# A one-core embedding, attention and expert kernel: first group's rows gathered apart, embeddings moved to later slots, squares in halves, first expert weights rounded in quarters

## What is computed

```python
emb = word_table[ids] + (domain_table[dom] @ proj_w.T + proj_b) + type_table[kind] + pos_table[pos]
h = layer_norm(emb, gamma, beta)                      # 32 sequences x 128 tokens x 192
x = layernorm(h)                                      # "magnitude" attention, 12 heads of 16
sr, si = (qr@kr + qi@ki) * scale, (qi@kr - qr@ki) * scale
h = h + softmax(sqrt(sr*sr + si*si)) @ v
h = h + causal_attention(layer_norm(h)) @ proj + b    # ordinary causal attention
h = h + mixture_of_experts(layer_norm(h))             # 8 experts, top 2, capacity 1280 rows each
```

## Time and profile before

| | |
|---|---|
| median of 3 runs | 1126.58 us (1125.38 to 1136.05) |
| the profiled execution | 1129.93 us |
| its span, first to last instruction | 1128.1 us |
| busy, share of the span | PE 83%, weight loads 63%, ACT 60%, DVE 59%, POOL 41% |
| mean granted TensorE clock | 0.908 of full speed |

### The profile page before, as it was taken

One profiled execution on the slowest core, in us unless ns is written; L12 is line 12 of the kernel. 1 busy time (PEld: TensorE's weight loads), 2 busy tenths in 40 slices (PEclk: granted clock), 3 DMA queues, 4 the chain that ended last, 5 costly groups with the idle time before them and its releaser, 6 DMA issues.

```text
span 1128.1 us, 21988 instructions
## 1 busy us (share of the span) xinstructions
PE 934.3 (83%) x7210; PEld 713.2 (63%) x7210; DVE 665.4 (59%) x3058; ACT 673.0 (60%) x1339; POOL 464.4 (41%) x508
## 2 busy tenths in 40 slices
PE   1234888879888979999999999946999999999996
PEld 1222555556555556666666666535888888889896
DVE  1344889879887766676766656374433434433332
ACT  2013888877888877887787778435443443443431
POOL 6666465444000110223222212213476676676654
PEclk7565999999999969999999998655999999999999
DMA  7233232232011100011011012143473455474352
GB/s 196 42 59 54 58 66 38 50 60 37 19 29 24 35 2 1 2 34 34 2 34 34 4 32 62 34 82 34 88 110 68 89 110 75 78 114 74 53 56 28
DMA packets 64259, 59.23 MB, mean 53 GB/s; under 512 B 17534, under 2 KB 55328, under 8 KB 64160
## 3 DMA queue, kind: packets, MB, share of 16 engines
q0 software_dynamic: 26112, 27.89, 18.0%
q1 hardware_dynamic: 38048, 30.12, 10.3%
HBM read 35.28 MB, written 16.39 MB: 46 GB/s over the span
## 4 chain that ended last, share of the span: by engine, by line
PE 55%; DVE 14%; ACT 11%; issue 7%; POOL 6%; DMA 4%; SPq 2%; ACTq 0%; POOLq 0%; DVEq 0%
PE ps_scores L724 13%; PE ps_ring L716 9%; PE ps_ring L965 7%; PE ps_ring L724 6%; POOL got L547 4%; PE ps_scores L965 4%; PE ps_scores L839 4%; ACT square L1061 3%; PE ps_ctx L856 3%; PE ps_scores L842 3%; SPq L458 2%; DVE probs L1329 2%; DMA got<-place_rows,id_now 2%; PE ps_ring L796 1%; ACT prob_t L1054 1%
## 5 line engine op out<-in xcount | busy, mean ns | idle before, releaser
L598 POOL DMA_INDIRECT out<-z_t,slots_now x80 | 135.3, 1692 | 102.1 <-DVE z_t L1624 83.0
L1168 ACT ACTIVATE probs<-ps_scores,fc_bias 128x512 f32<-128x512 f32 (+1 forms) x144 | 88.3, 617 | 146.9 <-PE ps_scores L724 143.7
L1054 ACT ACTIVATE prob_t<-ps_ring 128x512 f32<-128x512 f32 x192 | 113.8, 595 | 34.9 <-PE ps_ring L716 32.9
L716 PE MATMUL ps_ring<-ident,probs 128*128 128x128 f32 x768 | 127.8, 292 | 5.6 <-DVE x_hi L1222 2.5
L1061 ACT ACTIVATE square<-ps_scores 128x1024 f32<-128x1024 f32 x96 | 98.3, 1024 | 45.5 <-PE ps_scores L839 44.3
L1329 DVE CUSTOM_DVE_ANT_0 probs<-ps_scores,causal 128x128 f32<-128x128 f32 x384 | 88.8, 286 | 58.4 <-PE ps_scores L842 58.0
L1077 ACT ACTIVATE probs<-probs,neg_max 128x128 f32<-128x128 f32 x384 | 120.7, 395 | 3.6 <-DVE neg_max L1329 3.6
L965 PE MATMUL ps_ring<-work,probs 128*128 128x192 f32 x672 | 115.9, 328 | 5.6 <-ACT probs L1168 5.4
L1323 DVE CUSTOM_DVE_ANT_0 probs<-square 128x128 f32<-128x128 f32 x384 | 89.0, 286 | 46.2 <-ACT square L1061 43.1
L965 PEld LDWEIGHTS ps_ring<-work,probs 128*128 128x128 f32 x672 | 109.2, 190 | 9.4 <-issue 9.4
L724 PE MATMUL ps_scores<-x_hi,fc_hi 128*128 128x512 f32 (+1 forms) x288 | 105.1, 370 | 7.4 <-DVE x_hi L1608 4.8
(11 more groups left out here) (211 smaller groups left out, 2207.3 us busy)
## 6 DMA issues: line engine op xcount, KB each, us to landing
k<-k_signed SPq DMA_DIRECT2D x192, 32.0 KB
work<-pj_w SPq DMA_DIRECT2D x8, 576.0 KB, 4.4
token_in<-xin SPq DMA_DIRECT2D x8, 384.0 KB, 3.5
out<-resid SPq DMA_DIRECT2D x8, 384.0 KB, 4.3
vals<-fc_w SPq DMA_DIRECT2D x8, 384.0 KB, 3.4
vals<-fc_w SPq DMA_DIRECT2D x16, 192.0 KB, 4.2
out<-z_t,slots_now POOLq DMA_INDIRECT x80, 3.6
token_in<-xin SPq DMA_DIRECT2D x8, 128.0 KB, 4.3
```

The costliest lines, as they stand in the source:

```text
L598: gp.indirect_dma_start(out[:, :], bass.IndirectOffsetOnAxis(slots_now[:, u, 1, t:t + 1], 0), slot_y[:, o, :], None, compute_op=ALU.add).t ...
L716: return pe.transpose(dst, src, ident[0:n, 0:n])
L1054: sc.activation(prob_t[:, s % 2, :, :], src.rearrange("p (h q) -> p h q", h=4), ACT.Exp if p is mag else ACT.Copy).then_inc(ring_free[i], 1)
L1168: sc.activation(hidden[:, c % 2, f_, 0:128 * nt], ps_scores[:, i, 0:128 * nt], ACT.Gelu, bias=fc_bias[:, e, f_:f_ + 1]).then_inc(gelu_done ...
```

## The change

It does eight things. (1) The first group's position and domain rows are gathered without adding, into the two halves of the `square` tile, so no kind waits for the one before; DVE adds the three together (two 128x768 additions). (2) `id_now` has two buffers and the word gathers of the next group no longer wait for the last domain rows. (3) SP loads the causal weights only once the first group's domain rows have landed. (4) `EMBED_LATE` moves DVE's embedding steps of groups 1, 2, 3, 4 later by 9, 9, 5 and 2 slots, their "xT" fills with them, and gives group 1 its projections at slots 9 to 13 of pass 0. POOL's norms move to slots 4 and 6 for groups 0 and 1, and to slots 4 and 12 for all others. (5) The first group's keys are moved with 8 DMAs of all three blocks instead of 24. (6) ACT squares each job in two instructions of two heads, each with its own wait and its own release. (7) The first expert's weights are rounded and their remainder made in quarters, in slots 3 to 6 and 5 to 8 of pass 16. (8) `LAST_LAGS` is one slot later for all but "keep".

```diff
-XT_SLOT = {"mag": (0, 1), "cau": (1, 2)}
+XT_SLOT = {"cau": (1, 2)}
+EMBED_LATE = (0, 9, 9, 5, 2, 0, 0, 0)
+EARLY_PROJ, EARLY_VALUE = {1: (9, 10, 10, 11, 12, 13)}, {0: (14, 15), 1: (14, 15)}
-SPLIT_SLOT = 4
+SPLIT_SLOT = 3
+def magnitude_fills(at, g):
+    fills = back_fills(at - STEPS)
+    first = max(0, EMBED_LATE[g] - 2)
+    fills += [("xT", k) for k in range(2) if at == first + k - STEPS]
+    fills += [("proj", k) for k in range(6) if at == EARLY_PROJ.get(g, MAG_PROJ)[k] - STEPS]
+    return fills + [("value", k) for k in range(2) if at == EARLY_VALUE.get(g, MAG_VALUE)[k] - STEPS]
+def embedding_due(p, slot):
+    for g in range(GROUPS):
+        at = STEPS * (p - g + 2) + slot - EMBED_LATE[g]
+        if 4 <= at <= 13:
+            return g, at
+    return None, None
-LAST_LAGS = {"ctx": 4, "ctxT": 5, "out": 7, "scale": 7, "norm": 9, "zT": 10, "keep": 11, "logits": 12}
+LAST_LAGS = {"ctx": 5, "ctxT": 6, "out": 8, "scale": 8, "norm": 10, "zT": 11, "keep": 11, "logits": 13}
...
+                if done is cau_w_loaded:
+                    sp.wait_ge(dom_got, 16 * GROUP)
...
-            for g in range(GROUPS):
+            sp.wait_ge(keys_signed, BLOCKS)
+            for quarter, part in product(range(4), range(2)):
+                to, of = 32 * quarter + HEAD_DIM * part, 32 * quarter + HEAD_DIM * (1 - part)
+                sp.dma_start(k_of[0][to:to + HEAD_DIM, :, 1, :, :].rearrange("p b s k -> p b (s k)"),
+                             k_signed[of:of + HEAD_DIM, :, :]).then_inc(first_turned, 16)
+            for g in range(1, GROUPS):
...
                 if slot == 0:
-                    if g > 0:
-                        pool.wait_ge(dom_got, 16 * GROUP * g)
                     if g > 1:
+                        pool.wait_ge(dom_got, 16 * GROUP * (g - 1))
                         pool.wait_ge(mag.named("emb_affine0"), g)
...
-                    if slot == 4:
+                    if slot == 4 and g == 0:
+                        pool.wait_ge(place_stored, 16 * KINDS)
+                    elif slot == 4:
                         pool.wait_ge(word_got, 16 * GROUP * (g + 1))
-                        if g == 0:
-                            pool.wait_ge(place_stored, 16 * KINDS)
-                    gather(place_rows, g, slot - 4, place_got, 2, ALU.add)
+                    if g == 0:
+                        gather(apart_from_word[0], place_rows, g, slot - 4, place_got, 2, ALU.bypass)
+                    else:
+                        gather(place, place_rows, g, slot - 4, place_got, 2, ALU.add)
...
             def embedding_norm(p, g, slot):
-                first, second = (2, 5) if p < 0 else (5, 11)
+                first, second = (4, 6) if g < 2 else (4, 12)
...
-                act.wait_ge(mag.scores_full, 2 * (JOBS * g + j) + 2)
-                sc.activation(square[:, j % 2, :, :, :].rearrange("p h m k -> p h (m k)"),
-                              ps_scores[:, :, 0:256], ACT.Square).then_inc(mag.scores_free, 2)
+                for pair in range(2):
+                    act.wait_ge(mag.scores_full, 2 * (JOBS * g + j) + pair + 1)
+                    h = slice(2 * pair, 2 * pair + 2)
+                    sc.activation(square[:, j % 2, h, :, :].rearrange("p h m k -> p h (m k)"),
+                                  ps_scores[:, h, 0:256], ACT.Square).then_inc(mag.scores_free, 1)
...
+            def first_weights_high(quarter):
+                act.wait_ge(raw_loaded, 48)
+                c, some = quarter // 2, slice(FF // 2 * (quarter % 2), FF // 2 * (quarter % 2) + FF // 2)
+                sc.activation(fc_hi[:, 0, c, some], raw_fc[:, c, some], ACT.Copy).then_inc(first_high, 1)
...
-                    if (p, slot) == (2 * GROUPS, SPLIT_SLOT):
-                        expert_weights_high(0, 0)
+                    if p == 2 * GROUPS and 0 <= slot - SPLIT_SLOT < 4:
+                        first_weights_high(slot - SPLIT_SLOT)
...
                 if slot == 4:
+                    if g == 0:
+                        dve.wait_ge(word_got, 16 * GROUP)
+                        rows_, whole = got[:, 0:GROUP * HID], (place_got, dom_got)
+                        for u in range(2):
+                            dve.wait_ge(whole[u], 16 * GROUP)
+                            ve.tensor_tensor(rows_, rows_, first_got[u], ALU.add).then_inc(rows_added, 1)
+                            dve.wait_ge(rows_added, u + 1)
...
-                    if coming is not None and coming < GROUPS:
-                        embedding_step(coming, slot)
-                    elif coming is not None:
+                    g, at = embedding_due(p, slot)
+                    if g is not None:
+                        embedding_step(g, at)
+                    if coming is not None and coming >= GROUPS:
                         causal_input_step(coming - GROUPS, slot)
```

60 lines of the change are left out of this document (39 added, 21 removed).

## The result

| kernel | median, us | of runs | ratio to before | 95% interval |
|---|---|---|---|---|
| before | 1125.98 | 4 | | |
| changed | 1110.73 | 4 | 0.9858 | 0.982 to 0.9896 |

The change makes the kernel faster by 15.3 us, 1.4%. The forecast was a gain of 33 us; 1110.73 lies 0.7 us above the upper end of its range.

A forecast was written before the change was run, and what follows sets the result against it. No engine fills a steady pass; waits around a loop set it, DVE nearest to a bound, and a chain of waits delays the start. -38 + 5 + 10 - 10.5 + 0 = -33.5 us, predicted 1093, range 1078 to 1110.

The forecast's parts named there:

- First group's rows: Ahead of pass 0: last gather starts at 20.9, group 0's statistics at 26.7 instead of 33.8, PE's first product at 41.0.
- Group 0's keys: Ahead of pass 0: last signed copy at 47.3, eight key DMAs landed at 54.9, so scores may start at 55.
- rival C: Group 0's key DMAs: 8 with three times the issue time, scores not before 65; total 1100 us, chance 0.09.
- Pass 0: First magnitude pass: first maximum at 58.0, length 34.3 us, pass 1's at 92.3 instead of 130.4; gain 38, bounds 32 and 43.
- What the later passes give back: Passes after pass 0 and the end: effects of lateness +5, POOL's order +10, halved squares -10.5, the end 0 us.
- (a): After pass 1's first maximum: about 5 us of postponed DVE work is paid back as the lateness falls from 9 to 0.
- (b): POOL's second norm behind the gathers: 13 us of DVE waits in later passes, 10 of them lost; bounds 0 and 15.
- (c): Squares by halves: seven passes gain 1.5 us each, 10.5 together; bounds 0 and 3 a pass, 1 lost at worst.
- (d): The end: weight rounding in quarters and the last group's later lags change 0 us, bounds -1 and +2.
- A: Rival: the gather order on POOL costs nothing; gain 43.5 us, total 1083, chance 0.17.
- B: Rival: halves bring nothing and all waits for POOL's norms bite in full; gain 18 to 22 us, total 1106, chance 0.20.
- D: Rival: DVE's new waits idle PE, its clock falls to 1.2 GHz in magnitude passes; slower, 1144 us, chance 0.02.

The follow-up runs named there:

- the run with the norm early: On the changed kernel, POOL's second norm of groups 2 to 7 at slot 8, ahead of the next group's domain gathers, instead of slot 12: 1104.8 us.

## Why the prediction was wrong, point by point

**First group's rows: right, 1.7 late.** Gathers at 0.95 and 0.30 of issue, the last at 21.2. The statistics came at 28.4 for 26.7: DVE's weight remainders lasted until 26.5 here (24.5 taken over from the earlier trace rows), and only then came the additions, which took 1.94 for the 2.2 taken and waited for no landing. The remainders came late because ACT rounded the weights 2.0 later than before, at 22.2 for 20.2:

```profile
22.24 1.48 ACT L1037 ACTIVATE w_hi<-probs 128x1536 fp32r<-128x1536 f32 x1 [10.49 <-issue]
```

SP issued the loads of these weights only 0.4 later (15.3 for 15.0); where the other 1.6 went was not tried.

**Group 0's keys: 3 us more.** 15 products took until 50.2 with the last copy, for 47.3: 1.6 of it from the start, the rest from a slow clock that lasted from 42.6 to 47.8 and not 3.5 us. The eight DMAs took 5.24, 0.65 each, so rival C (three times the issue for three times the size) is out. But the last of them took 4.43 to land where the 32 KB one of the earlier trace rows took 3.15, 1.3 of the 4.4 by which the keys were late. The Trainium skill (DMA: Bandwidth & Descriptors, Anatomy of one DMA — SWDGE (gpsimd) path) fits 2.0 us and bytes over 436 GB/s to transfers issued from GpSimd; for 96 KB that is 2.2 us, an estimate. These transfers are from SP, and 4.43 was measured on them: the fit does not carry over.

**Pass 0: the step that failed.** "With the 4.5 us that DVE idles in a steady pass, and 1 for the slower clock, it lasts 34.3." It lasts 41.6: 7.3 of the 17.7 that are missing. The sum took the busy time of the engine that is busiest in a steady pass and added the steady pass's idle. But between the jobs of pass 0 DVE does not set the pace, it idles 10.7 of 29.8: PE is busy 26.9, and scores and squares give the first jobs one every 1.7 to 2.6 us. The tail of 11.8 follows in any case. The shortest intervals and the shortest tail of passes 0 to 6 of all the kernels, though of passes with other work, would make 34.6 together, more than the 34.3. Without the early products the pass is 37.3. The other 4.3 are the early products of group 1 between the last jobs (intervals of 3.6, 3.2 and 6.1); that is shown by a run. The other 3.0 are argued from the rows: PE and ACT pace the jobs there, and how much of that is the clock, for which the sum has 1, stays open. I had counted PE's work as at most 29.6 and looked no further, and it came to 33.2; 3.2 of the 3.6 come with the halves alone (32.8 in pass 0 of that run). The view that would have told this is the windows of the earlier trace rows cut once more, at the last job's maximum.

**What the later passes give back.** Forecast -5, -10 and +10.5 from pass 1 on, together -4.5; measured 27.4 at pass 1 and 15.8 at the first causal maximum, -11.6. Of the terms: (a) DVE's payback 5, measured 4.9. (b) POOL's order 10, measured 6 (the run with the norm early): DVE waits 4.1 in passes 1 and 3, where 5.5 and 3.7 stood, and not in pass 4. (c) the halves 10.5, measured 11.1 by the median of the run without them and 8.8 by that of the halves alone; in passes 1 to 7 of the traces 9.6 and 5.9. What no term held is the rest of the lateness: 17.5 minus 4.9 minus 5.6 is 7.0 us of waits in passes 1 to 3, a term that the sum does not have. 4.4 of them go with less lateness once POOL's order is mended, by one pair of traces, and 2.4 by another. PE's part in them is seen in pass 1: the late fill of the transposed input stands in mid-pass ahead of scores, PE waits with DVE (4.2), and the granted clock is 0.86 in place of 1.00. (d) 0, measured 0. So (b) was put 4 us too high, which by luck covered part of the missing 7.0.

ACT's side of the halves came cheaper than I had it. Group by line of the changed kernel (count, busy us, mean ns, idle before):

```profile
L1101 ACT ACTIVATE square<-ps_scores 128x512 f32<-128x512 f32 x192 | 104.8, 601 | 29.0 <-PE ps_scores L877 25.3
```

96 squares of 1.02 make 98.3, so 96 more instructions cost 6.5 us, not the 16 of my rows: of two halves back to back the second begins before the first has ended. By their mean the 192 halves sum to 115.4, and ACT is busy 104.8: an overlap of 0.11 a pair. The Trainium skill (ScalarE: Activation LUTs, What ACT_TABLE_LOAD costs) has back-to-back instructions overlap by about 93 ns, and the estimate of 9 from it was nearer; the trace agrees with the overlap.

**The rivals.** A (POOL's order is free) is refuted by the 4.1 us waits. B came closest in its number (1106), and by luck: it had the halves bring nothing, and they brought more than any other part that was tried. C is out, as said. D holds in a small way: the clock of passes 1 to 3 is 0.86, 0.96 and 0.92 where it was 1.00, 1.00 and 0.97, but no pass of these fell to the lower level.

**The median.** I took before's profiled execution to be 3.3 above its median and carried that through. That was right (3.95), and the changed kernel's lay at its median.

**The range.** By the prediction's own terms, B with the slow bound of pass 0 is a gain of 32 - 5 - 15 = 12, so the upper end should have been 1115 and not 1110. The measured time lies under that, which says little: the wide range came from doubts about the clock and group 2's rows, not about the pace between the jobs.

**The signs.** Pass 1's first maximum came at 103.1, past the 98 that was to show me wrong. The second norm cost DVE 8.2 us in passes 1 and 3 for the 13 in three passes. Its wait for squares fell from 29.7 to 21.7 in 272 us from pass 1 on, not under 20. Pass 1's clock was 0.86, under the 0.9. Passes 5 and 6 took 37.2 and 37.9, near the 37 that I gave, and pass 7 42.1.

## What to carry to other kernels

Cut a pass at its inner joints, not only at its ends, before you shorten it by an engine's busy time: work taken off the busiest engine counts only in the stretch that this engine paces, and between the jobs of pass 0 PE was busy 26.9 of 29.8 us and DVE 19.1. When work is made late so that the first pass may start early, every queue in which it now stands behind something else hands a part back; 18 us of an earlier first maximum became 5 in the traces and 4 by the medians. And look in both traces at a stretch that the change does not touch: here 5.1 us of a difference of 20.9 lay in such a one, as much as some of the parts that were to be measured.
